# A graph kernel's first stage: last rank round cut short, layer norm moved to VectorE, triangles moved to Pool, order planned anew

## The chip, the cores and the metric

The kernel runs on one core of one Trainium2 chip. The metric is the device time of one execution in microseconds.

## What is computed

There are 16 graphs of 1024 nodes with 128 features each, a weighted adjacency matrix per graph and a node mask. Two layers follow each other, and each adds its result to x:

```python
h = jnp.maximum(_layernorm(x, axis=-1), 0.0)
x = x + L0(h, adj)               # three times: h = h@W+b; nh = h/|h|; cos = nh@nh.T; h = (adj*cos)@h; relu but for the last
h = jnp.maximum(_layernorm(x, axis=-1), 0.0)
x = x + L1(h, adj, nodemask)     # three graph convolutions with adj * keep, batch norms, a last product

def step(carry, n):              # keep comes from this scan over the 1024 rows of (adj > 0)
    row = jnp.take(carry, n, axis=0); nbi = row.astype(jnp.int32); num = jnp.sum(nbi)
    sf = jnp.where(num > T_DIL, (num + K_DIL - 1) // K_DIL, 1)      # T_DIL = 10, K_DIL = 2
    rm = row & (jnp.cumsum(nbi) % sf == 0)
    keep = ~jnp.where((mask_b[n] != 0) & (num > 1), rm, False)
    carry = carry.at[n].set(row & keep)
    carry = carry.at[:, n].set(carry[:, n] & keep)
```

The scan doesn't depend on x. It removes neighbours by rank, and each removal changes later rows.

## The kernel before

The first stage (`layer0`, lines 474 to 1021) does two things side by side.

**The convolutions.** 48 units (16 graphs times three products). Graphs go in pairs, two units alternating. A unit has 16 cosine steps and 16 aggregate steps, each on a half row block of 128x512: TensorE makes three cosine matmuls into one of two PSUM banks (lines 702 to 704), VectorE multiplies by the adjacency into one of four buffers (line 889), TensorE aggregates (line 711). Between them the next unit is prepared: for the first of a graph the layer norm, in three steps: `lna` (statistics on VectorE, lines 852 to 855, and a square root on ScalarE, line 759), `lnb` (reciprocal and -mean/deviation on VectorE, lines 859 and 861, then eight ScalarE instructions x*scale+bias, line 767), `lnc` (transposes on TensorE, line 639, and ReLU on ScalarE, line 778). For every unit then `ha` (line 683), `hb` (line 869), squares (line 784), `hc` (lines 873 and 789), `hd` (reciprocal, line 877, and eight ScalarE scalings, line 794), `hf` (transposes, line 639, and a copy, line 801), `ho` (line 881).

**The dilation.** The scan in blocks of 128 rows: 4 quads of 4 graphs, 8 blocks each, so 32 blocks n; two chains of 16 blocks (even and odd quads) run interleaved. In a block the removals of the diagonal 128x128 part are iterated a fixed number of rounds, `ROUNDS = [2, 3, 4, 6, 6, 3, 3, 8]` for the eight blocks (35 a quad). First the rows are loaded, ScalarE takes their sign (`row`, line 815), and a transposing DMA fills the slab T. `cross` (lines 921 and 925, VectorE) makes the matrix X from the triangle of the row block (Au) and from T. `base` counts (TensorE line 721, VectorE lines 939 and 941). A round r is: `rank` (TensorE line 734, into bank D0), `rule` (nine small VectorE instructions, lines 953 to 967), `rank` on ScalarE (four instructions, line 822), `drop` (VectorE, line 974), which writes one of the two buffers Sd. After the last round come `bias` (VectorE), eight `wide` steps (TensorE line 744 into bank D1, ScalarE line 832 into v, VectorE line 1006 into T), and `check` (line 1000), which compares the two Sd buffers and adds what differs to a flag; a flag above 0 starts a repair loop on the device, `dilate_all`. `flip` and `mask` (line 1018) make the keep matrix of a quad and store it.

**The order.** A planner (`Planner.order`) gets every step with engine, cost in ns, rank and predecessors (`plan_units`, `plan_dilation`), simulates all engines greedily (earliest start first, lower rank first) and writes one fixed order per engine. Each engine runs its list in that order and waits on semaphores at the head of its queue. Pool has no work in this stage. The second stage (lines 1256 on) follows after a barrier.

Of the kernel before, what the change touches and what calls it, by code (L numbers as in the profile page):

```python
# [9 lines left out]
BF16 = mybir.dt.bfloat16  # L10
# [3 lines left out]
ALU = mybir.AluOpType  # L14
# [23 lines left out]
ENGINES = ("pe", "act", "dve", "sp", "dma")  # L38
TAIL = {"pe": 60, "act": 130, "dve": 90, "sp": 0, "dma": 2000}
# [65 lines left out]
def build(nc, A):  # L105
    with ExitStack() as top:
# [7 lines left out]
        C["U2"] = sb("U2", [128, 132], BF16)  # L114
# [42 lines left out]
def setup(nc, A, C):  # L157
    with ExitStack() as ctx:
# [23 lines left out]
        def dve(e):  # L182
# [4 lines left out]
            e.memset(C["U2"][:], 1.0)  # L187
# [23 lines left out]
            e.tensor_scalar(C["U2"][:, 0:128], t[:, 1, :], 2.0, None, ALU.mult)  # L211
# [16 lines left out]
class Planner:  # L228
# [16 lines left out]
    def order(self, rings):  # L245
# [25 lines left out]
        for _ in range(len(steps)):  # L271
# [21 lines left out]
            if s.frees:  # L293
                ring, key = (s.frees, s.name) if s.frees in rings else (s.frees[0], s.frees)
                free[ring][held[(ring,) + key]] = s.end
# [20 lines left out]
def plan_units(P):  # L316
# [10 lines left out]
    def prepare(v):  # L327
# [4 lines left out]
        if i == 0:  # L332
# [17 lines left out]
        add("act", ("hd", v), 1610, 0, [("dve", "hd", v)])  # L350
# [14 lines left out]
    def agg(idx):  # L365
# [10 lines left out]
        if i == 2 and idx % 16 == 11:  # L376
            read = [("act", "lnb", G)] if g == G - 1 else []
            transfer(("xload", g), 1400, read + ([("dma", "postb", UNITS.index((g - 1, 2)))] if g else [("act", "lnb", 1)]))
# [10 lines left out]
    add("dve", ("lnb", G), 400, 1, [("act", "lna", G)])  # L389
    add("act", ("lnb", G), 1610, 1, [("dve", "lnb", G), ("pe", "hf", 3 * G - 1)])  # L390
    add("act", ("first", 0), 920, 3, [("act", "lnb", G)])
# [14 lines left out]
def plan_dilation(P):  # L406
# [3 lines left out]
    for n in sorted(range(QUADS * NK), key=lambda n: (n // NK // 2 * NK + n % NK, n // NK % 2)):  # L410
# [16 lines left out]
        if k:  # L427
# [3 lines left out]
        add("dve", ("cross", n), 1330, 5, ready + filled +  # L431
            ([("dve", "check", prev)] if done else []))
        add("pe", ("base", n), 700, 1, ready, None, "D1")
        add("dve", ("base", n), 320, 2, [("pe", "base", n)], None, None, "D1")
        for r in range(K):
            add("pe", ("rank", n, r), 260, 1, [("dve", "drop", n, r - 1)] if r else ready, None, "D0")
            add("dve", ("rule", n, r), 1140, 3, [("pe", "rank", n, r)] + ([] if r else [("dve", "base", n)] + done))
            add("act", ("rank", n, r), 1365, 1, [("dve", "rule", n, r)], None, None, "D0")
            add("dve", ("drop", n, r), 610, 3, [("act", "rank", n, r)] + ([] if r else [("dve", "cross", n)]))
        add("dve", ("bias", n), 700, 3, [("dve", "rule", n, K - 1)])  # L440
        add("dve", ("check", n), 610, 6, [("dve", "drop", n, K - 1)])
        for i in range(Q):
            for j in range(2):
                add("pe", ("wide", n, i, j), 330, 1, [("dve", "drop", n, K - 1)], None, "D1")
                add("act", ("wide", n, i, j), 960, 1, [("pe", "wide", n, i, j), ("dve", "bias", n)], None, "v", "D1")
                add("dve", ("wide", n, i, j), 605, 4, [("act", "wide", n, i, j)], None, None, "v")
        for m, j in FLIPS:
            if k == max(2 * m + 1, 4 * j + 3):
                for i in graphs_of(quad):
                    transfer(("flip", quad, i, m, j), 600, [("dve", "wide", quad * NK + b, i, m // 2)  # L450
                             for b in range(4 * j, 4 * j + 4)], "flip", "flip", rank=2)
                    for q in (2 * m, 2 * m + 1):
                        last = ("flip", quad, i, m, j) if q % 2 else None
                        add("dve", ("mask", quad, i, q, j), 620, 3, [("dma", "flip", quad, i, m, j),
# [19 lines left out]
def layer0(nc, A, C, S):  # L474
    with ExitStack() as ctx:
        P = Scope(nc, ctx, "a", C["bank"][0])
        E = P.sems("w xl xld xs tln relu ph hr sq cl nrm rn vn tnh nh nl cos ew agg ev tpost xadd "
                   "bst bag lnsd lnrs lnm lnr " + " ".join(f"adj{i}{k}" for i in range(2) for k in range(NK)))
        T = P.sems("at0 at1 fl0 fl1 fl2 fl3 af0 af1 af2 sign low au x bs b0 b1 ct ru vr sd v8 wb wd av rw kp kps0 kps1 kps2 sum tot flag")
# [14 lines left out]
        lnnm = P.sb("lnnm", [128, NK])  # L494
# [8 lines left out]
        Au = P.sb("Au", [128, Q, 128], FP8)  # L503
# [4 lines left out]
        cnt, quarter = ([P.sb(f"{n}{p}", [128, Q]) for p in range(2)] for n in ("cnt", "quarter"))  # L508
# [3 lines left out]
        small = P.sb("small", [128, 2, 8, Q])  # L512
        sm = [{n: small[:, p, x, :] for x, n in enumerate(("sf", "iv", "g", "sc", "va", "h", "c", "b2"))}
              for p in range(2)]
        D0, D1 = P.ps("D0", [128, Q, 128]), P.ps("D1", [128, Q, 128])
# [1551 lines left out]
```

## Time and profile before

| | us |
|---|---|
| median of 3 runs | 2694.39 |
| lowest and highest | 2693.61, 2701.42 |
| the profiled execution | 2693.11 |
| its span in the trace | 2691.3 |

The span is the time from the first to the last instruction; 1.8 us lie around it. Engines: PE is TensorE's matmuls, PEld its weight loads (they overlap PE), DVE is VectorE, ACT ScalarE, POOL GpSimd, SP the queue that issues the DMAs. A group of instructions has its line, engine, operation, output<-input names and shapes, count, then busy us and mean ns of one, then the idle time of the engine just before them and what ended it. Instructions of one engine overlap by some tens of ns, so that eight of them take less than eight times their mean.

### The profile page before, as it was taken

To read this page: it belongs to the slowest core of one execution; us is meant where nothing else is said; L and a number is where in the kernel's file an instruction comes from. 1 tells how busy PE (TensorE), PEld (TensorE's weight loads), DVE (VectorE), ACT (ScalarE), POOL (GpSimd) and SP (SyncE) were. 2 spreads that over 40 slices of the span, in tenths; PEclk is the share of its full clock that TensorE was granted. 3 is DMA by queue.
4 is the path that set the end of the run, shared out by engine and by line. 5 is a ranking of instruction groups with operands and counts; after the bars stand their busy time and mean duration, and the time that the engine had idled before them with its cause. 6 is when DMAs were issued, how large, how long until landed. Compare 5 with 4: busy or idle time off the path is not lost. (4 is left out here: it accounts for less than half of the span.)

```text
span 2691.3 us, 38914 instructions
## 1 busy us (share of the span) xinstructions
PE 2579.7 (96%) x12390; PEld 1630.3 (61%) x12390; DVE 2076.1 (77%) x5328; ACT 1459.3 (54%) x4324; POOL 562.7 (21%) x233
## 2 busy tenths in 40 slices
PE   6999999999999999899999998999999999999898
PEld 4666656656655666566666654555555555555897
DVE  4778889888988888888988877766666636776676
ACT  5667747766655776567656321322322344443676
POOL 0000000000000000000000002766666603433673
PEclk9999999999999999999999999999999999999999
DMA  7354275265367244536433323555555419996663
GB/s 235 89 148 147 57 187 156 65 160 167 77 170 220 83 136 133 128 100 192 114 112 120 83 69 140 195 191 192 193 192 192 182 55 384 404 402 263 249 233 153
DMA packets 325878, 455.48 MB, mean 169 GB/s; under 512 B 155680, under 2 KB 218528, under 8 KB 325664
## 3 DMA queue, kind: packets, MB, share of 16 engines
q1 hardware_dynamic: 325664, 452.89, 51.9%
q8 instruction: 102, 1.67, 0.3%
q14 instruction: 112, 0.92, 0.1%
HBM read 352.13 MB, written 67.11 MB: 156 GB/s over the span
## 5 line engine op out<-in xcount | busy, mean ns | idle before, releaser
L711 PE MATMUL a_acc<-a_ew,a_Hr 128*128 128x512 f32 x1536 | 751.9, 600 | 0.5 <-ACT a_hT L807 0.4
L889 DVE TENSOR_TENSOR a_ew<-adj,a_cos 128x512 f32<-128x512 f32 x768 | 508.6, 682 | 68.3 <-PE a_cos L704 66.0
L1720 POOL TENSOR_TENSOR b_dsum<-adj 128x1024 f32<-128x1024 f32 x15 | 133.3, 8885 | 1797.4 <-DVE adj L1628 1797.4
L702 PE MATMUL a_cos<-a_nh 128*128 128x512 f32 x768 | 413.3, 538 | 14.0 <-DVE a_ew L889 7.3
L711 PEld LDWEIGHTS a_acc<-a_ew,a_Hr 128*128 128x128 f32 x1536 | 275.2, 190 | 160.7 <-issue 112.2
L832 ACT ACTIVATE a_v<-a_D,a_wb,a_small 128x256 f16<-128x256 f32 x512 | 287.8, 635 | 86.4 <-PE a_D L744 84.5
L704 PE MATMUL a_cos<-a_nh,a_nl 128*128 128x512 f32 x768 | 304.1, 396 | 0.0
L703 PE MATMUL a_cos<-a_nl,a_nh 128*128 128x512 f32 x768 | 301.6, 393 | 0.0
L822 ACT ACTIVATE a_vr<-a_D,a_small 128x128 f16<-128x128 f32 x560 | 209.4, 456 | 135.3 <-DVE a_small L967 134.7
L1383 PE MATMUL b_acc<-adj,b_z 128*128 128x512 f32 x512 | 225.0, 592 | 0.0
L1480 PE MATMUL b_acc<-adj,b_z 128*128 128x512 f32 x512 | 222.5, 592 | 0.0
L815 ACT ACTIVATE a_Ab<-stage 128x512 fp8e4<-128x512 f32 x256 | 156.7, 633 | 111.2 <-DMA stage<-in_adj 110.5
L1724 POOL TENSOR_TENSOR b_dsum<-b_dsum,adj 128x1024 f32<-128x1024 f32 x90 | 211.4, 2349 | 12.9
L702 PEld LDWEIGHTS a_cos<-a_nh 128*128 128x128 f32 x768 | 145.5, 189 | 101.4 <-issue 44.1
L1018 DVE TENSOR_TENSOR a_kp<-a_T,stage 128x512 fp8e4<-128x512 fp8e4 x256 | 170.0, 686 | 41.4 <-DMA scr_keep<-a_kp 39.2
L1006 DVE SCALAR_TENSOR_TENSOR a_T<-a_v,a_Ab 128x512 fp8e4<-128x512 f16 x256 | 172.2, 685 | 29.0 <-ACT a_v L832 28.6
L703 PEld LDWEIGHTS a_cos<-a_nl,a_nh 128*128 128x128 f32 x768 | 146.3, 191 | 64.2 <-issue 51.4
L1480 PEld LDWEIGHTS b_acc<-adj,b_z 128*128 128x128 f32 x512 | 96.0, 190 | 114.3 <-issue 113.1
L704 PEld LDWEIGHTS a_cos<-a_nh,a_nl 128*128 128x128 f32 x768 | 144.7, 188 | 33.4
L1383 PEld LDWEIGHTS b_acc<-adj,b_z 128*128 128x128 f32 x512 | 94.8, 190 | 107.1 <-issue 107.1
L784 ACT ACTIVATE h<-a_Hr 128x128 f32<-128x128 f32 x384 | 113.1, 299 | 69.2 <-DVE a_Hr L869 69.1
L1515 ACT ACTIVATE b_z<-b_o 128x128 f32<-128x128 f32 x256 | 75.3, 297 | 116.9 <-DVE b_o L1699 100.6
(269 smaller groups left out, 4337.6 us busy)
## 6 DMA issues: line engine op xcount, KB each, us to landing
adj<-in_adjT SPq DMA_DIRECT2D x108, 1024.0 KB, 12.8
adj<-in_adjT SPq DMA_DIRECT2D x128, 512.0 KB, 4.3
stage<-in_adj SPq DMA_DIRECT2D x256, 256.0 KB, 3.3
scr_keep<-a_kp SPq DMA_DIRECT2D x256, 64.0 KB, 1.8
scr_z<-b_zT SPq DMA_DIRECT2D x32, 512.0 KB, 3.6
scr_ag<-b_a SPq DMA_DIRECT2D x32, 512.0 KB, 3.3
stage<-scr_keep SPq DMA_DIRECT2D x13, 1024.0 KB, 7.5
b_kp<-scr_keep SPq DMA_DIRECT2D x12, 1024.0 KB, 7.8
```

The costliest lines, as they stand in the source:

```text
L702: e.matmul(cos[j][:], n[:, blk(k)], n[:, half(j)], start=True, stop=False)
L703: e.matmul(cos[j][:], n[:, blk(k)], m[:, half(j)], start=False, stop=False)
L704: e.matmul(cos[j][:], m[:, blk(k)], n[:, half(j)], start=False, stop=True).then_inc(E["cos"], 1)
L711: e.matmul(acc[j][:], Hr[u % 2][:, k, :], ew[idx % EW][:], start=(k == 0), stop=(k == NK - 1)).then_inc(E["agg"], 1)
L822: e.activation(vr[p][:, i, :], D0[:, i, :], ACT.Abs, bias=sm[p]["b2"][:, i:i + 1], scale=sm[p]["sc"][:, i:i + 1]).then_inc(T["vr"], 1)
L832: t = e.activation(v[c % 3][:, g * 256:g * 256 + 256].rearrange("p (x s) -> p s x", s=2), D1[:, 2 * g:2 * g + 2, :], ACT.Abs, bias=wb[p][: ...
L889: e.tensor_tensor(ew[idx % EW][:], adj[g % 2][:, k, half(j)], cos[j][:], ALU.mult).then_inc(E["ew"], 1)
L1006: e.scalar_tensor_tensor(TT[:, slot, 2 * j:2 * j + 2, k].rearrange("p m x s -> p m (x s)"), v[c % 3][:].rearrange("p (m c) -> p m c", m=2) ...
L1018: e.tensor_tensor(as_blocks(kp[c % 3][:]), row_half(slot, j, q), turned[:, :, :, :, q % 2], ALU.mult, saturate=False).then_inc(T["kp"], 1)
L1383: t = e.matmul(acc[j][:], src[:, q, :], adj[n % 3][:, q, half(j)], start=(q == 0), stop=(q == NK - 1))
L1480: t = e.matmul(acc[j][:], z[m % 2][:, q, :], adj[slot(m)][:, q, half(j)], start=(q == 0), stop=(q == NK - 1))
L1724: e.tensor_tensor(d, d, b[:, q, :], ALU.add).then_inc(E["ds"], 1)
```

## The change

- The last round of a block has its rank product and its rule, but no ScalarE ranks and no removal: the rule's count and scale go straight into `wide`, which reads the Sd of the round before. `wide` needs the drop of round K-2; D0 is given back by the rule. The check runs after the block's wide steps: a new VectorE instruction makes the K-th Sd from the diagonal block of T that the wide step wrote, and the old instruction compares it with the other.
- `lnb`: the eight ScalarE instructions become eight VectorE `tensor_scalar` (subtract mean, multiply by 1/deviation); line 861 goes.
- The triangle (line 921) becomes a Pool `tensor_tensor`, with two buffers Au instead of one.
- U2 goes, UL stands in its place; `cnt` and `quarter` lie in `small`. The repair loop is adapted.
- The planner gets Pool as an engine and new costs: `lnb` 2280 ns on VectorE (before 400 there and 1610 on ScalarE), `hd` on ScalarE 2340 (1610), `row` 540 (620), `cross` 610 (1330) and `tri` 1250 on Pool, `check` 1220 (610), `mask` 605 (620). The orders of all engines come out anew.

```diff
-ENGINES = ("pe", "act", "dve", "sp", "dma")
-TAIL = {"pe": 60, "act": 130, "dve": 90, "sp": 0, "dma": 2000}
+ENGINES = ("pe", "act", "dve", "pool", "sp", "dma")
+TAIL = {"pe": 60, "act": 130, "dve": 90, "pool": 150, "sp": 0, "dma": 2000}
...
-            add("dve", ("lnb", g), 400, 1, [("act", "lna", g)])
-            add("act", ("lnb", g), 1610, 0, [("dve", "lnb", g)] + ([("pe", "hf", 0)] if g == 1 else []))
-            add("pe", ("lnc", g), 880, 0, [("act", "lnb", g)] + bank)
+            add("dve", ("lnb", g), 2280, 1, [("act", "lna", g)] + ([("pe", "hf", 0)] if g == 1 else []))
+            add("pe", ("lnc", g), 880, 0, [("dve", "lnb", g)] + bank)
...
-        add("act", ("hd", v), 1610, 0, [("dve", "hd", v)])
+        add("act", ("hd", v), 2340, 0, [("dve", "hd", v)])
...
-                add("act", ("row", n, i, j), 620, 2, [("dma", "row", n, i, j)], None, None, "af")
+                add("act", ("row", n, i, j), 540, 2, [("dma", "row", n, i, j)], None, None, "af")
...
-        add("dve", ("cross", n), 1330, 5, ready + filled +
-            ([("dve", "check", prev)] if done else []))
+        add("pool", ("tri", n), 1250, 1, [("act", "row", n, i, k // 4) for i in range(Q)] +
+            ([("dve", "cross", prev)] if done else []))
+        add("dve", ("cross", n), 610, 5, ready + filled + [("pool", "tri", n)] + ([("dve", "check", prev)] if done else []))
...
-            add("act", ("rank", n, r), 1365, 1, [("dve", "rule", n, r)], None, None, "D0")
-            add("dve", ("drop", n, r), 610, 3, [("act", "rank", n, r)] + ([] if r else [("dve", "cross", n)]))
+            if r < K - 1:
+                add("act", ("rank", n, r), 1365, 1, [("dve", "rule", n, r)], None, None, "D0")
+                add("dve", ("drop", n, r), 610, 3, [("act", "rank", n, r)] + ([] if r else [("dve", "cross", n)]))
...
-        add("dve", ("check", n), 610, 6, [("dve", "drop", n, K - 1)])
+        add("dve", ("check", n), 1220, 6, [("dve", "wide", n, i, k // 4) for i in range(Q)])
...
-                add("pe", ("wide", n, i, j), 330, 1, [("dve", "drop", n, K - 1)], None, "D1")
+                add("pe", ("wide", n, i, j), 330, 1, [("dve", "drop", n, K - 2)], None, "D1")
...
+        def pool(e):
+            for kind, *a in plan["pool"]:
+                n, = a
+                k, p, prev = n % NK, n // NK % 2, block_before(n)
+                e.wait_ge(T["sign"], max(nth["act", "row", n, i, k // 4] for i in range(Q)))
+                if prev is not None:
+                    e.wait_ge(T["x"], nth["dve", "cross", prev])
+                mine = Ab[:, slots(n), 256 * (k // 2):256 * (k // 2) + 256].rearrange("p i (x s) -> p i x s", s=2)
+                e.tensor_tensor(Au[p][:], mine[:, :, :, k % 2], C["tri"][:].unsqueeze(1).to_broadcast([128, Q, 128]),
+                                ALU.mult, saturate=False).then_inc(T["au"], 1)
...
-                    for k in range(NK):
-                        t = e.activation(tmp[:, k, :], x[:, k, :], ACT.Identity, bias=lnnm[:, k:k + 1],
-                                         scale=lnrs[:, k:k + 1])
...
-                    e.scalar_tensor_tensor(lnnm[:], lnmv[:, :, 0], -1.0, lnrs[:], ALU.mult, ALU.mult).then_inc(E["lnm"], 1)
+                    if g in (1, G):
+                        e.wait_ge(E["tnh"], 3 * g if g == G else 1)
+                    for k in range(NK):
+                        t = e.tensor_scalar(tmp[:, k, :], x[:, k, :], lnmv[:, k, 0:1], lnrs[:, k:k + 1],
+                                            ALU.subtract, ALU.mult)
+                    t.then_inc(E["lnr"], 1)
...
-                    e.wait_ge(T["sd"], nth["dve", "drop", n, ROUNDS[n % NK] - 1])
+                    k, p, c = n % NK, n // NK % 2, nth["dve", "check", n]
+                    e.wait_ge(T["rw"], max(nth["dve", "wide", n, i, k // 4] for i in range(Q)))
+                    e.wait_ge(T["ct"], nth["pe", "rank", n, ROUNDS[k] - 1])
+                    e.scalar_tensor_tensor(Sd[p][ROUNDS[k] % 2][:], TT[:, slots(n), k // 2, k, :, k % 2], 0.0, X[p][:],
+                                           ALU.is_equal, ALU.is_lt, saturate=False).then_inc(T["again"], 1)
```

## Rows read from the trace of the kernel before

**Rows 1.** The page: busy time by engine, and granted clock in 40 slices.
```profile
PE 2579.7 (96%) x12390; PEld 1630.3 (61%) x12390; DVE 2076.1 (77%) x5328; ACT 1459.3 (54%) x4324; POOL 562.7 (21%) x233
...
PEclk9999999999999999999999999999999999999999
```

**Rows 2.** Busy time by stretch: PE, PEld, DVE, ACT, POOL, clock, DMA share, GB/s.
```profile
0.00:30.18 30.18, 7.69 (x32) 6.62 (x33) 7.93 (x44) 13.47 (x40) 1.54 (x9) 1.00 0.82 302
30.18:1626.60 1596.42, 1539.72 (x7690) 978.94 (x7690) 1358.15 (x3645) 1004.94 (x2803) 0.00 (x0) 1.00 0.46 127
1626.60:2691.30 1064.70, 1032.28 (x4668) 644.75 (x4668) 710.05 (x1639) 440.87 (x1481) 561.19 (x224) 0.99 0.61 228
```

**Rows 3.** Waits of PE in 0 to 1625 us: total us, times, longest us.
```profile
PE a_pp L639 <- ACT h L767: 25.6, 16, 12.0
PE a_pp L639 <- ACT h L794: 18.7, 16, 7.0
PE a_D L744 <- ACT a_v L832: 11.4, 8, 3.6
PE a_cos L702 <- DVE a_ew L889: 7.3, 10, 1.3
PE a_cos L702 <- DVE a_nl L881: 6.0, 9, 2.4
PE a_D L721 <- DVE a_T L905: 2.5, 2, 1.3
...
PE a_D L734 <- DVE a_Sd L974: 0.8, 3, 0.3
```

**Rows 4.** Groups of instructions of the first stage, by line.
```profile
L889 DVE TENSOR_TENSOR a_ew<-adj,a_cos 128x512 f32<-128x512 f32 x768 | 508.6, 682 | 68.3 <-PE a_cos L704 66.0
...
L815 ACT ACTIVATE a_Ab<-stage 128x512 fp8e4<-128x512 f32 x256 | 156.7, 633 | 111.2 <-DMA stage<-in_adj 110.5
...
L974 DVE SCALAR_TENSOR_TENSOR a_Sd<-a_vr,a_X 128x512 fp8e4<-128x512 f16 x140 | 96.1, 686 | 27.0 <-ACT a_vr L822 26.8
...
L767 ACT ACTIVATE h<-h,a_lnnm,a_lnrs 128x128 f32<-128x128 f32 x120 | 47.8, 481 | 22.1 <-DVE a_lnnm L861 22.1
...
L921 DVE SCALAR_TENSOR_TENSOR a_Au<-a_Ab,tri 128x512 fp8e4<-128x512 fp8e4 x32 | 21.9, 685 | 0.9 <-DMA a_T<-a_Ab 0.9
```

**Rows 5.** Instructions in order of time, the start: start us, us, instruction, [idle before].
```profile
8.52 0.17 DVE L861 SCALAR_TENSOR_TENSOR a_lnnm<-a_lnmv,a_lnrs 128x8 f32<-128x8 f32 x1
8.72 3.18 ACT L767 ACTIVATE h<-h,a_lnnm,a_lnrs 128x128 f32<-128x128 f32 x8 [0.47 <-DVE a_lnnm L861]
...
11.96 1.97 PE L639 MATMUL a_pp<-ident,h 128*128 128x128 f32 x8 [11.96 <-ACT h L767]
```

**Rows 6.** Instructions in order of time, three places of the steady part.
```profile
651.41 3.19 ACT L767 ACTIVATE h<-h,a_lnnm,a_lnrs 128x128 f32<-128x128 f32 x8 [2.32 <-DVE a_lnnm L861]
654.50 1.48 ACT L822 ACTIVATE a_vr<-a_D,a_small 128x128 f16<-128x128 f32 x4
...
654.65 1.09 PE L639 MATMUL a_pp<-ident,h 128*128 128x128 f32 x8 [1.22 <-ACT h L767]
...
1584.77 2.45 ACT L794 ACTIVATE h<-a_Hr,a_rnrn 128x128 f32<-128x128 f32 x8 [1.09 <-DVE a_rnrn L877]
```

**Rows 7.** Instructions in order of time, VectorE in the second stage.
```profile
1656.72 2.14 DVE L1614 TENSOR_SCALAR xt<-xt,b_lnmv,b_lnrs 128x128 f32<-128x128 f32 x8
1658.78 9.16 DVE L1628 TENSOR_TENSOR adj<-adj,b_kp 128x1024 f32<-128x1024 f32 x8
```

**Rows 8.** Single lines of the second stage: duration ns min/median/max, first and last start.
```profile
L1679 DVE TENSOR_TENSOR b_rm<-b_rnrn,mf x16: 167/1970/1973, 1673.3 to 2173.1; 128x8 f32<-128x8 f32 x16
...
L1720 POOL TENSOR_TENSOR b_dsum<-adj x15: 8875/8882/8942, 1661.2 to 2133.5; 128x1024 f32<-128x1024 f32 x15
...
L1724 POOL TENSOR_TENSOR b_dsum<-b_dsum,adj x90: 2338/2348/2397, 1670.3 to 2154.9; 128x1024 f32<-128x1024 f32 x90
```

**Rows 9.** Instructions in order of time: two long waits of TensorE.
```profile
348.03 1.97 PE L639 MATMUL a_pp<-ident,h 128*128 128x128 f32 x8 [3.17 <-ACT h L794]
...
544.54 0.63 ACT L815 ACTIVATE a_Ab<-stage 128x512 fp8e4<-128x512 f32 x1 [4.22 <-DMA stage<-in_adj]
...
547.74 0.49 PE L744 MATMUL a_D<-UL,a_T 128*128 128x256 bf16 x4 [3.20 <-ACT a_v L832]
```

**Rows 10.** Busy time by stretch, columns as in rows 2.
```profile
345.00:350.00 5.00, 1.97 (x9) 1.85 (x10) 3.47 (x6) 3.97 (x11) 0.00 (x0) 0.75 0.53 132
```

**Rows 11.** The check's line, columns as in rows 8.
```profile
L1000 DVE SCALAR_TENSOR_TENSOR a_Au<-a_Sd x32: 682/685/693, 66.6 to 1488.3; 128x512 fp8e4<-128x512 fp8e4 x32
```

More of the change, by code:

```diff
@@ L113, in build @@
         C["tri"] = sb("tri", [128, 128], FP8)
-        C["U2"] = sb("U2", [128, 132], BF16)
         C["UL"] = sb("UL", [128, 512], BF16)
@@ L293, in order @@
             if s.frees:
-                ring, key = (s.frees, s.name) if s.frees in rings else (s.frees[0], s.frees)
+                ring, key = (s.frees, s.name) if s.frees in rings else s.frees
                 free[ring][held[(ring,) + key]] = s.end
@@ L376, in agg @@
         if i == 2 and idx % 16 == 11:
-            read = [("act", "lnb", G)] if g == G - 1 else []
-            transfer(("xload", g), 1400, read + ([("dma", "postb", UNITS.index((g - 1, 2)))] if g else [("act", "lnb", 1)]))
+            read = [("dve", "lnb", G)] if g == G - 1 else []
+            transfer(("xload", g), 1400, read + ([("dma", "postb", UNITS.index((g - 1, 2)))] if g else [("dve", "lnb", 1)]))
     transfer(("xfirst", 1), 1400, (), "sp")
@@ L452, in plan_dilation @@
                     for q in (2 * m, 2 * m + 1):
-                        last = ("flip", quad, i, m, j) if q % 2 else None
-                        add("dve", ("mask", quad, i, q, j), 620, 3, [("dma", "flip", quad, i, m, j),
+                        last = ("flip", ("flip", quad, i, m, j)) if q % 2 else None
+                        add("dve", ("mask", quad, i, q, j), 605, 3, [("dma", "flip", quad, i, m, j),
                             ("dve", "wide", quad * NK + q, i, j)], f"flip{quad}{i}{m}{j}", "kp", last)
@@ L502, in layer0 @@
         Ab = P.sb("Ab", [128, 2 * Q, N], FP8)
-        Au = P.sb("Au", [128, Q, 128], FP8)
+        Au = [P.sb(f"Au{p}", [128, Q, 128], FP8) for p in range(2)]
         X = [P.sb(f"X{p}", [128, Q, 128], FP8) for p in range(2)]
@@ L515, in layer0 @@
         D0, D1 = P.ps("D0", [128, Q, 128]), P.ps("D1", [128, Q, 128])
+        cnt, quarter = ([small[:, p, x, :] for p in range(2)] for x in (8, 9))
         mv4 = C["mv"][:].rearrange("p (g k) -> p g k", k=NK)
@@ L652, in take @@
                         e.wait_ge(T["b0"], nth["dve", "base", a[0]])
+                    elif kind == "rank" and a[1] == ROUNDS[a[0] % NK] - 1:
+                        e.wait_ge(T["ru"], 9 * nth["dve", "rule", a[0], a[1]])
                     elif kind == "rank":
@@ L857, in dve @@
                     g, = a
+                    x = xt if g in (1, G) else tmp
                     e.wait_ge(E["lnsd"], g + 1)
@@ L1019, in dve @@
                                     saturate=False).then_inc(T["kp"], 1)
-        run(nc, pe, act, dve, None, sp)
+        run(nc, pe, act, dve, pool, sp)
 def dilate_all(nc, A, C, S):
@@ L1045, in rule @@
             m = mv[:, k:k + 1]
-            e.tensor_tensor(cnt[:], Dp[:, 0, 128:129], base[:, 1:2], ALU.add).then_inc(E["rule"], 1)
+            e.scalar_tensor_tensor(cnt[:], Dp[:, 0, 128:129], 0.5, base[:, 1:2], ALU.mult, ALU.add).then_inc(E["rule"], 1)
             e.wait_ge(E["rule"], t0 + 1)
@@ L1070, in recount @@
             e.wait_ge(E["sd"], 1)
-            e.matmul(Dp[:, 0, 0:129], Sd[:], C["U2"][:, 0:129], start=True, stop=True).then_inc(E["rank"], 1)
+            e.matmul(Dp[:, 0, 0:129], Sd[:], C["UL"][:, 0:129], start=True, stop=True).then_inc(E["rank"], 1)
         with nc.Fori(0, G) as g:
@@ L1111, in pe @@
                                  start=(q == others[0]), stop=(q == others[-1]))
-                    e.matmul(Dp[:, 0, 0:129], AT[:, k, blk(k)], C["U2"][:, 0:129], start=True,
+                    e.matmul(Dp[:, 0, 0:129], AT[:, k, blk(k)], C["UL"][:, 0:129], start=True,
                              stop=True).then_inc(E["rank"], 1)
```

59 lines of the change are left out of this document (21 added, 38 removed).

## The prediction

> **What bounds the kernel now.** I read the page first: TensorE is busy 96% of the span, the other engines far less, and the granted clock is at its upper level nearly all the time [rows 1]. The change touches only the first stage, so the next view is the busy time by stretch: it cuts the run into the start, the steady part of the first stage (from the first cosine product at 30.18 us to the last store's transposes at 1626.6 us) and the rest [rows 2]. In the steady part TensorE works 1539.7 of 1596.4 us. The change adds no matmul and removes none: the ranks of the last round stay, and the move from U2 to UL keeps the same 128 columns. So what it can win is in the 56.7 us in which TensorE stands still there, plus the start, where it works 7.7 of 30.2 us. Third, the waits of TensorE by line [rows 3]. They say which engine was late: the transposes (L639) waited 25.6 us for the layer norm's output from ScalarE (L767) and 18.7 us for the normalised rows (L794). The wide products (L744) waited 11.4 us for L832. VectorE is behind the cosine waits, 7.3 and 6.0 us. The longest of these waits, 12.0 and 7.0 us and 2.4 of the cosine waits on L881, are the start. Steady, L767 costs 25.6 - 12.0 = 13.6 us in 15 waits, L794 18.7 - 7.0 = 11.7 us in 15. The rest of the first stage is bound by TensorE's own work, and everything after 1626.6 us is untouched.
>
> **Why those waits are there.** All engines of this stage follow orders that a planner wrote from its own costs, so a step that takes longer than its cost is waited for at the head of TensorE's queue. The layer norm's second half is entered at 400 ns on VectorE and 1610 ns on ScalarE, but the eight ScalarE instructions take 3.19 us [rows 6], 1.58 more. At 651 us they end at 654.6 and the transposes start then, after 1.22 us of standing still [rows 6]; an average wait of 13.6 / 15 = 0.9 us fits a shortfall of 1.58. L794 is also entered at 1610 ns and takes 2.45 us [rows 6], 0.84 short.
>
> **The change, part by part.**
> Start. The first layer norm is a bare chain. Now the small product at 8.52 us is followed by 3.18 us on ScalarE and TensorE starts at 11.96 [rows 5]. After, eight VectorE instructions with two per-row scalars follow the reciprocal, where the small product stood. The same instruction form with the same shapes stands in the second stage: eight in 2.14 us [rows 7]. Start 8.52, end 10.66, TensorE at about 10.75: **-1.2 us**. One conversion of U2 and one fill less in the setup: 0 to -0.15, take -0.1.
>
> Layer norm, steady. On ScalarE 17 x 3.19 = 54 us go [rows 4, 6]. On VectorE 17 x 2.14 = 36.4 us come, less 17 small products of 0.17 (one at the start is in [rows 5]), 2.9 us. The new entry, 2280 ns, is near 0.20 + 0.04 + 2.14 = 2.38 us, so the shortfall of 1.58 falls to 0.1. The order can then put cosine and aggregate products ahead of the transposes. Bounds: 0 back (the wait only changes its name) to 13.6 back. I take **-11**, since the cause is one constant error that is repaired.
>
> The hd entry, 1610 to 2340 ns. It alone repairs the L794 waits. Of the 11.7 us, 3.17 come from one wait in another situation (a ScalarE instruction behind a late load, below), so 8.5 are open. Bounds 0 and 8.5; I take **-6.5**.
>
> Last round without ranks and removal. Each of the 32 blocks loses four ScalarE instructions (4 of them in 1.48 us at 654.5 us [rows 6]): 47 us of ScalarE in all, and one removal of 0.69 us on VectorE [rows 4], 22 us. The check gets it back as one more instruction of the same shape, 22 us: nothing on VectorE. The chain of a block gets shorter by 1.48 + 0.69 + two crossings, about 2.3 us; 16 blocks follow each other in either of the two chains, so the last check, now at 1488 us [rows 11], comes up to 37 us earlier. Nobody on TensorE waits for it: the stage ends with the aggregates at 1626 us. Worth 0 by itself. The wide products can start before the last rule is done but their reader L832 can't, so D1 may be held about 1.5 us longer by the first of eight. That touches base products and other wide products that share D1. Bounds: 32 x 1.5 = 48 us of a held bank if TensorE always stood in front of it, and below nothing, since ScalarE, with 101 us less to do, is late less often. TensorE's waits on L832 are 11.4 us in 8, with two of 3.2 and 3.6 us. The one of 3.2 us: ScalarE waits 4.22 us for a load of adjacency rows, then L832 comes late, then L744 [rows 9]. Such waits come from loads, not from ScalarE's work, and a new order deals them anew; I leave them in number. They also cost clock: after the 3.17 us wait before 348 us [rows 9] the granted clock of the stretch is 0.75 [rows 10], that is part of it at the lower level of 1.2 GHz. For the smaller waits on L832 I take **-1**.
>
> Triangles on Pool. VectorE loses 32 x 0.684 = 21.9 us (L921) [rows 4]. Pool gets 32 instructions of 512 elements a partition. The nearest row is its two-input instruction on 1024 f32 elements, 2.35 us [rows 8]: half is 1.2 us. They start when the row signs are there and the crossing also waits for transposes behind those signs, so the result is early; Pool does nothing else in this stage. The price is elsewhere. In the second stage the small VectorE product L1679, with both inputs in SBUF, takes 0.17 us at least but 1.97 us in the median, where Pool is at work, and Pool's L1720 takes 8.9 us, not 2.35, as the eight products L1628 of two SBUF tiles run on VectorE [rows 7, 8]. So each triangle can hold VectorE for up to 1.2 us: 38 us in all. L889, 508.6 us [rows 4], has one operand in PSUM, and VectorE is idle 238 us of the steady part [rows 2]; together that is 47% of the time, so about half of the triangles meet something they hold, about 20 us. That eats what L921 gave back.
> The Trainium skill, page "SBUF — State Buffer", section "Who interferes with whom", speaks against this part: the pair of ports that VectorE and GpSimd share is an exclusive lock, and an instruction with two SBUF inputs, or a `tensor_scalar` in a two-port mode, blocks in full against a GpSimd instruction that reads SBUF. The rows just named agree with it ([rows 8]). By that rule the new layer norm instructions can be held too; the time it would give is rival 3's, worked out there from rows alone.
>
> VectorE as a whole: +36.4 - 2.9 - 21.9 = +11.6 us of work, and about 20 us of holding, on 1358 of 1596 us [rows 2]: from 85% to 87%. What TensorE pays for VectorE now is 7.3 + (6.0 - 2.4) + 2.5 + 0.8 = 14.2 us steady [rows 3]. A layer norm step now blocks the queue for 2.4 us in one piece, ahead of the element products L889 that free the cosine banks; there are 768 of them in 1596 us, one in 2.08, each 0.68 us, so a block of 2.4 us is 1.0 more than the 1.4 between two of them. Bounds: 0, and 38 + 16 x 1.0 = 54 us. From the row it is nearest to (14.2 us paid at 85% load) I take **+5**.
>
> **Sum.** -1.2 - 0.1 - 11 - 6.5 - 1 + 5 = -14.8 us. The profiled execution took 2693.1 us (span 2691.3 and 1.8 around it), the median of the runs is 2694.4. Rounded for what a new order spoils, I take -14: **2680 us**, 0.5% faster. A measurement of this kernel tells 0.3%, 8 us, from no change.
>
> **Rivals.**
> (1) The forecast, 2672 to 2686 us: chance 0.48.
> (2) The waits change their names. The two repaired entries take 17 us of waiting away, but the new order meets its own late loads and late L832, as at 348 and 547 us [rows 9]. One such wait of 3.4 us with its slow clock (about 2 us more) is 5.5; two more of them and a cost of 5 to 10 us on VectorE give back 16 to 21, so 2688 to 2697. For it: ScalarE stood idle 111 us before its row signs, for loads [rows 4], and no entry for loads is changed. Against it: the average of such waits needn't grow. Chance 0.27.
> (3) Slower: Pool's triangles and the 2.4 us blocks hold L889. Place: VectorE's queue, where a held two-SBUF instruction stands ahead of an element product. Price: up to 38 us for the triangles and 16 for the blocks, against 20 won: at most +34, and at half of the price (27) plus two late loads (11) +18, 2712 us. It decides from about 0.9 us of each triangle reaching TensorE (32 x 0.9 = 29, against 20 won and past the 8 that can be told). Against it: VectorE is idle 15% of the time and four buffers of products lie between. Chance 0.11.
> (4) More: the stage closes up. With 101 us less on ScalarE and truer costs (the row entry goes from 620 to 540 ns too) most of the 56.7 us goes: 35 of it and 1.3 at the start, 2694 - 36 = 2658 us; partly, 2665. Chance 0.14.
> That the change doesn't do what it says: the check compares the same two rounds as before, so if nothing was unsettled before, nothing is now; otherwise the repair loop would run and cost far over 10%. Chance under 0.01, left out.
>
> **How the numbers follow.** Likeliest 2680. The forecast's own range is 2672 to 2686; to hold 8 in 10 it takes in rival 2 and the edges of 3 and 4: **2665 to 2698**. Faster by over 0.3% (below 2686.3): all of 1 and 4, 0.62. Within 0.3% (2686.3 to 2702.5): rival 2 and a little of 3, 0.29. Slower (above 2702.5): the rest of 3, 0.09.
>
> **What would show it.** In the profile after: the waits of L639 on the layer norm under 4 us steady and on L794 under 5; TensorE's first instruction near 10.8 us; ScalarE's first-stage work down by about 100 us; VectorE's up by 12 us plus held instructions (its two-SBUF instructions with maxima near 1.8 us); Pool with 32 instructions of about 1.2 us; the last check before 1460 us; the second stage unchanged at 1064.7 us. Wrong would be: waits of L702 on L889 over 20 us (rival 3), waits of L744 on L832 over 20 us (rival 2, or D1 held), or a second stage that moves by more than 3 us.

## The result and the profile after

The changed kernel takes 2690.7 us (median of 19 runs, 2683.4 to 2695.4), the kernel before 2696.6 in the same 19 rounds. The ratio is 0.998, 95% interval 0.9972 to 0.9987: 5.4 us faster (3.5 to 7.5), where 14 were forecast. Carried over to the 2694.4 us that the forecast started from, that is 2689 us. It lies inside the range of 2665 to 2698 us, but in rival 2's stretch, the one that the forecast called no change, and outside the likeliest case's 2672 to 2686. The interval leaves 1 out, so this pair of orders does differ, by less than half of the forecast. Of the kernel before's 19 executions one took 8152 us; such slow ones are left out of every ratio. The profiled execution has a span of 2684.3 us, 7.0 below that of before.

By stretch (columns as in rows 2), the answer to [rows 2]:

```profile
0.00:28.82 28.82, 7.70 (x33) 6.63 (x33) 9.45 (x49) 10.29 (x32) 1.55 (x9) 0.86 0.82 306
28.82:1621.56 1592.74, 1535.18 (x7690) 983.19 (x7691) 1378.35 (x3725) 915.66 (x2547) 36.80 (x32) 0.99 0.47 128
1621.56:2684.30 1062.74, 1031.57 (x4668) 644.91 (x4668) 695.15 (x1639) 439.99 (x1481) 560.46 (x224) 0.99 0.60 229
```

The start is 1.4 us shorter, the steady part 3.7 (1596.4 before), the rest 2.0. ScalarE works 89 us less in the steady part, VectorE 20 us more, Pool 36.8 us for 32 triangles. But TensorE stands still for 1592.7 - 1535.2 = 57.6 us there, against 56.7 before. The waits show what filled the place (TensorE, 0 to 1625 us: total us, times, longest), the answer to [rows 3]:

```profile
PE a_cos L712 <- DVE a_ew L895: 16.4, 16, 2.1
PE a_cos L712 <- DVE a_nl L887: 14.8, 10, 3.0
PE a_D L754 <- ACT a_v L832: 11.5, 14, 2.3
PE a_pp L647 <- DVE h L865: 11.5, 2, 10.6
PE a_pp L647 <- ACT h L794: 8.6, 6, 7.0
PE a_D L744 <- DVE a_Sd L974: 7.8, 12, 1.2
PE a_D L731 <- DVE a_T L911: 2.5, 4, 1.6
PE a_D L731 <- DVE a_T L915: 1.8, 3, 0.9
```

Without the start (10.6, 7.0 and 2.4 us of these), the waits for the layer norm are 0.9 us where 13.6 stood, those for L794 1.6 where 11.7 stood: 22.8 us went. The waits for VectorE, for element products, the low part nl, removals and T, are 16.4 + 12.4 + 7.8 + 2.5 + 1.8 = 40.9 where 14.2 stood: 26.7 us came. The start is the bare chain that was forecast (VectorE, then TensorE, in order of time), the answer to [rows 5]:

```profile
8.39 2.14 DVE L865 TENSOR_SCALAR h<-h,a_lnmv,a_lnrs 128x128 f32<-128x128 f32 x8
...
10.59 1.97 PE L647 MATMUL a_pp<-ident,h 128*128 128x128 f32 x8 [10.59 <-DVE h L865]
```

Two places show VectorE late (VectorE, Pool and TensorE in order of time). In the first a crossing, 0.69 us elsewhere, takes 1.58 us beside a triangle on Pool. The element products and nl stand behind it, and TensorE waits 3.03 us, of which the hold is 0.9:

```profile
1068.34 1.34 POOL L641 TENSOR_TENSOR a_Au<-a_Ab,tri 128x512 fp8e4<-128x512 fp8e4 x1 [26.12 <-ACT a_Ab L815]
...
1068.65 1.58 DVE L925 SCALAR_TENSOR_TENSOR a_X<-a_T,a_Au 128x512 fp8e4<-128x512 fp8e4 x1
1070.16 1.27 DVE L895 TENSOR_TENSOR a_ew<-adj,a_cos 128x512 f32<-128x512 f32 x2
1071.35 1.21 DVE L887 TENSOR_TENSOR a_nl<-a_pp,a_nh 128x1024 fp32r<-128x1024 f32 x1
...
1072.62 0.80 PE L712 MATMUL a_cos<-a_nh 128*128 128x512 f32 x1 [3.03 <-DVE a_nl L887]
```

In the second the new check, two instructions in one step, stands ahead of nl:

```profile
423.30 0.69 DVE L998 SCALAR_TENSOR_TENSOR a_Sd<-a_T,a_X 128x512 fp8e4<-128x512 fp8e4 x1
424.02 0.69 DVE L1004 SCALAR_TENSOR_TENSOR a_X<-a_Sd 128x512 fp8e4<-128x512 fp8e4 x1
...
424.64 1.22 DVE L887 TENSOR_TENSOR a_nl<-a_pp,a_nh 128x1024 fp32r<-128x1024 f32 x1
...
425.91 0.50 PE L712 MATMUL a_cos<-a_nh 128*128 128x512 f32 x1 [1.97 <-DVE a_nl L887]
```

### The profile page after: what moved, and what is told of

Read it like the earlier page. It is cut to its first block and busy times, and to the rows that moved or that the text cites. A ratio compares the mean times of both kernels' runs of the same rounds, so it can differ in the third digit from the quotient of the medians.

```text
span 2684.3 us, 38830 instructions
## 1 busy us (share of the span) xinstructions
PE 2574.4 (96%) x12390; PEld 1634.7 (61%) x12390; DVE 2082.9 (78%) x5413; ACT 1365.9 (51%) x4060; POOL 598.8 (22%) x265
## 5 line engine op out<-in xcount | busy, mean ns | idle before, releaser
L895 DVE TENSOR_TENSOR a_ew<-adj,a_cos 128x512 f32<-128x512 f32 x768 | 508.0, 681 | 69.0 <-PE a_cos L714 67.1
L712 PE MATMUL a_cos<-a_nh 128*128 128x512 f32 x768 | 417.2, 543 | 31.5 <-DVE a_ew L895 16.4
L641 POOL TENSOR_TENSOR a_Au<-a_Ab,tri 128x512 fp8e4<-128x512 fp8e4 x32 | 36.8, 1150 | 1367.2 <-ACT a_Ab L815 1367.2
L832 ACT ACTIVATE a_v<-a_D,a_wb,a_small 128x256 f16<-128x256 f32 x512 | 287.2, 632 | 99.8 <-PE a_D L754 59.9
L822 ACT ACTIVATE a_vr<-a_D,a_small 128x128 f16<-128x128 f32 x432 | 161.9, 457 | 134.1 <-DVE a_small L967 133.8
```

The costliest lines, as they stand in the source:

```text
L712: e.matmul(cos[j][:], n[:, blk(k)], n[:, half(j)], start=True, stop=False)
L822: e.activation(vr[p][:, i, :], D0[:, i, :], ACT.Abs, bias=sm[p]["b2"][:, i:i + 1], scale=sm[p]["sc"][:, i:i + 1]).then_inc(T["vr"], 1)
L832: t = e.activation(v[c % 3][:, g * 256:g * 256 + 256].rearrange("p (x s) -> p s x", s=2), D1[:, 2 * g:2 * g + 2, :], ACT.Abs, bias=wb[p][: ...
L895: e.tensor_tensor(ew[idx % EW][:], adj[g % 2][:, k, half(j)], cos[j][:], ALU.mult).then_inc(E["ew"], 1)
```

## The experiments

Theory A: the repaired waits are a real gain, and VectorE's new load gave most of it back. Theory B: a new order deals the waits anew, whatever the parts do. Each ratio is to the kernel before, run beside it. Any change of a cost makes the planner write all orders anew; such an order is called a deal below. Three runs (f1 to f3) keep an order as it stands instead. The steady part of each run, from its first cosine product to its last transposes, is called its units.

**What a new order alone is worth.** One planner constant, in the kernel before (l1, l2) and in the changed one (l3, l4):

```diff
-SIGNAL = 100
+SIGNAL = 105      # l1, l3; 95 in l2, l4
```

> The kernel before with the planner's signal time at 105 ns for 100, nothing else: the same instructions and nearly the same costs, but the greedy planner deals another order. It measures what a new order alone is worth. Theory B (much of every difference here is the deal of the order): off the kernel before by 0.3% or more either way (8 us). Theory A (differences come from what is moved and from costs): within 0.15%.

> The kernel before with signal time 95 ns. Theory B: off by 0.3% or more, and not by the same as with 105. Theory A: within 0.15% of before.

> The changed kernel with signal time 105 ns. Theory B: off the changed kernel (0.998) by 0.3% or more. Theory A: ratio 0.9965 to 0.9995.

> The changed kernel with signal time 95 ns. Theory B: off 0.998 by 0.3% or more, with the last mask anywhere between 1560 and 1640 us. Theory A: ratio 0.9965 to 0.9995.

Measured: l1 1.0044 (1.0027 to 1.0060), l2 1.0077 (1.0060 to 1.0093), l3 0.9957 (0.9941 to 0.9973), l4 0.9973 (0.9962 to 0.9983). The same instructions in another order cost 12 and 21 us. The old order is the best of its three deals, and theory B holds for it. The three deals of the changed kernel lie within 0.23%, less than theory B's 0.3%, though l3 lies just below theory A's 0.9965. The means are 1.0040 and 0.9970, 0.7% or 19 us apart. No deal of one side reaches the other's, but three a side are few: luck alone would part them in this way in one case of 20. In l2 the waits for the layer norm and L794 are there as in before (14.8 and 9.6 us), with 17.0 on L832.

**Costs alone.** e1 is the kernel before with four entries changed and no instruction moved, g3 the same with signal time 105 ns. The two entries not shown are `row` 540 and `mask` 605.

```diff
-            add("act", ("lnb", g), 1610, 0, ...
+            add("act", ("lnb", g), 3060, 0, ...
-        add("act", ("hd", v), 1610, 0, [("dve", "hd", v)])
+        add("act", ("hd", v), 2340, 0, [("dve", "hd", v)])
```

> The kernel before with nothing but truer planner costs: hd 2340 for 1610 ns, the layer norm's ScalarE half 3060 for 1610, row 540 for 620, mask 605 for 620; every instruction is that of before, only the orders are new. Theory A (the change gained through repaired costs, and VectorE's new load gave it back): the two waits of L639, 25 us steady before, fall under 6 and little comes back, 2679 to 2685 us, ratio 0.993 to 0.996. Theory B (a repaired wait returns under another name whatever carries it, since the new order deals the rest anew): the steady waits of TensorE sum to 45 to 60 us as before, ratio 0.998 to 1.001.

> The kernel before with true costs alone, second deal (105 ns). The first gave 1.0105. If true costs are worse in themselves: 1.007 to 1.013. If they are neutral against other deals of before (1.0044, 1.0077 and the kernel before itself, 1): 1.000 to 1.008. If the forecast's step holds (repaired entries gain 17 us): 0.993 to 0.998.

Measured: e1 1.0105 (1.0091 to 1.0120), g3 1.0098 (1.0070 to 1.0125), slower than every other deal of before, g3 as expected if true costs are worse in themselves. Theory A's expectation of 0.993 to 0.996 failed by 1.4%, and theory B's of 0.998 to 1.001 too. The two repaired waits did fall, to 2.1 and 6.0 us in e1, and came back with interest (TensorE in the units of e1; 2.4 us of the nl line are the start):

```profile
PE a_D L744 <- ACT a_v L832: 23.3, 17, 3.8
PE a_cos L702 <- DVE a_nl L881: 17.4, 10, 2.4
PE a_cos L702 <- DVE a_ew L889: 10.6, 16, 1.7
PE a_D L734 <- DVE a_Sd L974: 10.4, 12, 3.0
PE a_pp L639 <- ACT h L794: 6.0, 6, 2.8
```

TensorE waits 40.2 us for VectorE here, and 40.9 in g3, where it waits 14.2, 21.0 and 24.6 us in the three deals of before. VectorE's work is that of before. So the costs alone bring the waits for VectorE that the changed kernel shows (40.9).

**One entry back.** e5 is the changed kernel with the hd entry at 1610 again.

> The changed kernel with the one cost entry hd back at 1610 ns. Theory A (the repaired entry takes 8 to 10 us of waits away): L647 waits for L794 rise from 2 to 9 us or more in the steady part, ratio 0.999 to 1.002. If truer costs spoil more than they mend (before with true costs alone was 1.0%, and up to 0.6% worse than other orders of before): ratio 0.994 to 0.997. Theory B: 0.995 to 1.000 with no tie to the waits of L794.

Measured: 0.9967 (0.9954 to 0.9980), overlapping the changed kernel's own deals, and this (TensorE, from 28.9 us; 2.4 us of the nl line are the start):

```profile
PE a_pp L647 <- ACT h L794: 15.9, 23, 1.6
PE a_D L754 <- ACT a_v L832: 9.6, 12, 2.0
PE a_cos L712 <- DVE a_ew L895: 7.6, 10, 1.8
PE a_cos L712 <- DVE a_nl L887: 5.4, 5, 2.4
```

The wait for L794 is back as theory A expected, 15.9 us for 1.6 (3.5 and 1.5 in l3 and l4), but the ratio is not 0.999 to 1.002: it lies in the range for true costs that spoil more than they mend. The waits for nl and the element products are 10.6 us, where the changed kernel's three deals have 28.8, 20.7 and 17.0. L794, L801, L887 and the next unit's first cosine are one chain: with the transposes planned later, TensorE's wait goes from the chain's middle to its end. That fits these rows; it wasn't measured by itself.

**The layer norm.** f2 keeps the order of before; g5 and g6 (signal time 105) plan anew with the move alone; e2 and g1 (signal time 105) are the changed kernel with it back on ScalarE, -mean/deviation in `lnsd`.

```diff
# f2, g5, g6: on VectorE, after the reciprocal (g5, g6: one step of 2280 ns)
-                        t = e.activation(tmp[:, k, :], x[:, k, :], ACT.Identity, bias=lnnm[:, k:k + 1],
-                                         scale=lnrs[:, k:k + 1])
+                        t = e.tensor_scalar(tmp[:, k, :], x[:, k, :], lnmv[:, k, 0:1], lnrs[:, k:k + 1],
+                                            ALU.subtract, ALU.mult)
# e2, g1: the reverse in the changed kernel
-            add("dve", ("lnb", g), 2280, 1, ...
+            add("dve", ("lnb", g), 400, 1, [("act", "lna", g)])
+            add("act", ("lnb", g), 3060, 0, ...
```

> The order of the kernel before as it stands, but the layer norm's eight instructions are VectorE's, at the place of its small product; ScalarE's step is empty. The forecast's step (the waits of L639 on the layer norm go, 11 us, at little cost): ratio 0.995 to 0.997. If a 2.15 us block that the order didn't reckon with delays the element products: the 13 us come back as waits of L702, ratio 0.999 to 1.002.

> The kernel before with only the layer norm's move to VectorE and its cost of 2280 ns, planned anew. With the old order kept the move cost 0.23%. If the order has to reckon with the block for the gain to come, and the true value is 11 us against a typical deal of before (mean 1.004): ratio 0.997 to 1.002. If the move alone is worth nothing: 1.002 to 1.008.

> The kernel before with only the layer norm's move to VectorE, planned anew, second deal (105 ns). If a part has a value of its own, it repeats the first deal within 0.3%; if everything is the deal, it differs by 0.4% or more.

> The changed kernel with the layer norm's second half back on ScalarE, entered at its true 400 + 3060 ns. Theory A: the 36 us of VectorE blocks were what cost the wait for L881/L887 and the element products; without them these waits (28 us steady after the change) fall by about 10 us, 2682 to 2687 us, ratio 0.994 to 0.997. Theory B: within 0.15% of the changed kernel, ratio 0.997 to 1.000.

> The changed kernel with the layer norm's half back on ScalarE (true costs), second deal: signal time 105 ns. The first deal gave 1.0056. If the layer norm's place is worth its 0.8% in itself, this lies at 1.003 to 1.008, above all three deals of the changed kernel (0.9957 to 0.9980). If the first was a bad deal: 0.997 to 1.001.

Measured: f2 1.0023 (1.0014 to 1.0032), g5 1.0086 (1.0060 to 1.0112), g6 1.0082 (1.0064 to 1.0100), e2 1.0056 (1.0042 to 1.0070), g1 1.0011 (0.9996 to 1.0026). In f2 the waits for the layer norm went, but TensorE's wait of L734 for removals rose from 0.8 to 13.6 us, not those of L702 as expected: a block that the order doesn't reckon with. g5 looks like a loss and isn't one on TensorE (stretches of g5, columns as in rows 2):

```profile
28.98:1614.54 1585.56, 1539.38 (x7691) 980.83 (x7691) 1370.17 (x3729) 959.28 (x2675) 0.00 (x0) 0.99 0.45 126
1625.00:1650.00 25.00, 0.00 (x0) 0.00 (x0) 12.69 (x20) 0.00 (x0) 0.00 (x0) 0.50 0.37 92
```

Its units take 1585.6 us (g6: 1585.8), 10.9 less than before (l1 and l2: 1612.7 and 1619.8), and end at 1614.5. Then TensorE stands idle: VectorE still makes masks, the last at 1649.6 us, and the second stage's first VectorE instruction comes at 1658.8, where before had 1583.9 and 1635.5. A second path reaches the barrier, the dilation's; with the layer norm alone it ends last. The last check shows where it lost time: 1583.4 and 1585.8 us in g5 and g6, 1488.3, 1516.7 and 1544.5 in the three deals of before. g6 repeats g5 within 0.3%, but both lie above the 0.997 to 1.002 that a gain would have shown, since no expectation had this path. Back on ScalarE in the changed kernel the layer norm costs 0.3 to 0.8% in two deals (g1 lies between its two expectations); the units then take 1613.9 and 1598.9 us where the changed kernel's deals take 1592.2 to 1595.4, so its worth on TensorE shows from both sides. e2 missed both its expectations (0.994 to 0.997 and 0.997 to 1.000): taking the 2.15 us blocks off VectorE gained nothing.

**The short last round.** f3 keeps the order of before; e4 and g2 (signal time 105) are the changed kernel with the full round, the check's single comparison again behind the last removal.

```diff
# e4, g2 in the changed kernel
-            if r < K - 1:
-                add("act", ("rank", n, r), 1365, 1, [("dve", "rule", n, r)], None, None, "D0")
-                add("dve", ("drop", n, r), 610, 3, ...
+            add("act", ("rank", n, r), 1365, 1, [("dve", "rule", n, r)], None, None, "D0")
+            add("dve", ("drop", n, r), 610, 3, ...
-                add("pe", ("wide", n, i, j), 330, 1, [("dve", "drop", n, K - 2)], None, "D1")
+                add("pe", ("wide", n, i, j), 330, 1, [("dve", "drop", n, K - 1)], None, "D1")
```

> The order of the kernel before as it stands, without the last round's four ScalarE ranks and its removal; the check's instruction stays in its place but compares one Sd with itself and its result isn't used, so this kernel leaves the check out. It measures the shorter chain and 47 + 22 us less work with no new order. The forecast gave this 0 to -1 us: ratio 0.998 to 1.000. If the shorter chain is the gain that the variant with the full round pointed to (0.6% between it and the changed kernel): ratio 0.993 to 0.996.

> The changed kernel with the last round's four ScalarE ranks and its removal on VectorE restored, and the check's single comparison after it. Theory A: ScalarE has 47 us more to do, TensorE's waits on L832 (11.5 us) grow by a few us: ratio 0.998 to 1.001. If the check, now 1.4 us in one piece after the wide steps, is what delays the cosine chain on VectorE, this is faster, 0.995 to 0.997. The last check comes at 1488 us or later in the first case.

> The changed kernel with the full last round, second deal (105 ns). The first gave 1.0041, with the last mask at 1641 us, 20 us after TensorE's units: the dilation's chain set the stage's end. If the short last round is worth keeping the chain off the end, the last mask comes after 1615 us again and the ratio is 1.000 to 1.006. If that was the deal: last mask before 1600 and 0.996 to 0.999.

Measured: f3 0.9979 (0.9970 to 0.9988), e4 1.0041 (1.0028 to 1.0054), g2 1.0061 (1.0039 to 1.0083). f3's 6 us lie between both expectations; its profiled execution shows none of it (steady part 1597.4 us), so where they are stays open. e4 is slower than either of its expectations, and g2's masks end after 1615 us as expected. These two decide. TensorE's units take 1592.70 us in both, as in the changed kernel (1592.74): on TensorE the short round is worth nothing. But look at the mask's line (last start is the number before the semicolon) and the first VectorE instruction of the second stage: first changed kernel, then e4, then g5.

```profile
L1022 DVE TENSOR_TENSOR a_kp<-a_T,stage x256: 636/685/1418, 335.0 to 1573.3; 128x512 fp8e4<-128x512 fp8e4 x128
1630.05 0.17 DVE L1648 MEMSET onesf<- 128x128 f32 x1 [6.13 <-issue]
```

```profile
L1015 DVE TENSOR_TENSOR a_kp<-a_T,stage x256: 636/684/1501, 336.4 to 1640.9; 128x512 fp8e4<-128x512 fp8e4 x128
1649.38 0.17 DVE L1641 MEMSET onesf<- 128x128 f32 x1 [7.78 <-issue]
```

```profile
L1012 DVE TENSOR_TENSOR a_kp<-a_T,stage x256: 639/689/697, 342.2 to 1649.6; 128x512 fp8e4<-128x512 fp8e4 x128
1658.79 0.17 DVE L1638 MEMSET onesf<- 128x128 f32 x1 [8.53 <-issue]
```

With the full round the masks end 68 us later, 20 us behind the units, and the second stage starts 19 us later (g2: masks to 1645.3). The last check comes at 1566.9 and 1579.6 us in e4 and g2, at 1524.5 to 1534.3 in the changed kernel's three deals. So the short round is what lets the layer norm's move count.

**The triangle.** f1 keeps the order of the changed kernel and has VectorE make the triangle ahead of the crossing; e3 and g7 (signal time 105) plan anew. f1's order reckons with 610 ns on VectorE at that place, and the two instructions take 1.4 us.

```diff
# e3, g7 (f1 keeps the planned order)
-        add("pool", ("tri", n), 1250, 1, ...
-        add("dve", ("cross", n), 610, 5, ...
+        add("dve", ("cross", n), 1330, 5, ready + filled + ([("dve", "check", prev)] if done else []))
```

> The order of the changed kernel as it stands, instruction for instruction, but the triangle is made by VectorE at the place of the crossing and Pool does nothing. No new order, so only the place of the triangle is measured. If the hold through Pool costs more than the work: faster than the changed kernel, ratio 0.995 to 0.997. If the 22 us of VectorE work are worth more (rows of the changed kernel show only about 10 us of held instructions): ratio 1.000 to 1.003, that is 5 to 13 us over it. Theory B (what moves the time is the deal, parts are small): within 0.15% of 0.998.

> The changed kernel with the triangle back on VectorE (cost 1330 as before). If the hold through Pool's triangle costs more than the 22 us of work that it takes off VectorE, this is faster than the changed kernel: ratio 0.995 to 0.997, and VectorE's maxima fall to 0.69 us. If the move was worth its work, it is slower: ratio 0.999 to 1.002. Theory B expects no difference beyond 0.15% from 0.998.

> The changed kernel with the triangle on VectorE, planned anew, second deal (105 ns). The first deal gave 0.9958, the changed kernel 0.998, but with the changed kernel's order kept, the triangle on VectorE cost 0.3%. If the first deal was luck: 0.998 to 1.003. If the triangle is better on VectorE once the order reckons with it: 0.994 to 0.997.

Measured: f1 1.0012 (1.0002 to 1.0021), 0.32% or 8.6 us over the changed kernel; its steady part is 1600.4 us, 7.7 longer. e3 0.9958 (0.9946 to 0.9971), g7 1.0014 (1.0003 to 1.0025). By their expectations f1 says that the move was worth its work, e3 the opposite, and g7 that e3 was luck. In the order that was planned for Pool the triangle is better on Pool. With new orders TensorE sees no difference: the units take 1597.0 and 1592.5 us with the triangle on VectorE, 1592.7, 1595.4 and 1592.2 with it on Pool. What differs is the second path. The masks of e3 and of g7:

```profile
L1027 DVE TENSOR_TENSOR a_kp<-a_T,stage x256: 636/684/695, 331.0 to 1621.3; 128x512 fp8e4<-128x512 fp8e4 x128
```

```profile
L1027 DVE TENSOR_TENSOR a_kp<-a_T,stage x256: 640/686/694, 331.8 to 1628.9; 128x512 fp8e4<-128x512 fp8e4 x128
1637.87 0.17 DVE L1653 MEMSET onesf<- 128x128 f32 x1 [8.28 <-issue]
```

They end at 1621 and 1629 us, where the changed kernel's three deals have 1573.3, 1576.1 and 1587.8. In g7 that is 7.6 us behind the units, and its second stage starts 8 us later than the changed kernel's: about the 9 us of their ratios (1.0014 and 0.998). e3 and l3 (0.9957) are the fastest measured, but e3's second deal shows that as a draw of the order, not as a better design.

**All deals side by side.** Every kernel with an order of its own, in us of its profiled execution: how long TensorE stands idle in its units, what of it are waits for L794 and for VectorE (the layer norm apart), and where the last mask lies against the end of the units (minus: ahead of it).

| kernels | hd entry | layer norm | idle | for L794 | for VectorE | last mask |
|---|---|---|---|---|---|---|
| before, l1, l2 | 1610 | ScalarE | 56.7, 67.1, 73.6 | 11.7, 16.3, 9.6 | 14.2, 21.0, 24.6 | -43, -69, -39 |
| g5, g6 | 1610 | VectorE | 46.2, 49.7 | 6.4, 9.4 | 18.3, 15.5 | +35, +35 |
| e5 | 1610 | VectorE | 53.4 | 15.9 | 16.1 | -5 |
| e1, g3 | 2340 | ScalarE | 78.8, 73.0 | 6.0, 4.2 | 40.2, 40.9 | -33, -29 |
| e2, g1 | 2340 | ScalarE | 71.0, 57.2 | 1.7, 2.0 | 42.1, 25.1 | -75, -53 |
| changed, l3, l4 | 2340 | VectorE | 57.6, 54.2, 55.8 | 1.6, 3.5, 1.5 | 40.9, 26.4, 30.9 | -48, -48, -33 |
| e4, g2 | 2340 | VectorE | 54.8, 57.0 | 1.9, 6.1 | 33.0, 24.9 | +20, +24 |
| e3, g7 | 2340 | VectorE | 56.6, 53.9 | 3.1, 0.8 | 31.6, 36.1 | -4, +8 |

The waits for VectorE go with the hd entry: at 1610 they are 14.2 to 24.6 us in six deals, at 2340 they are 24.9 to 42.1 us in eleven, wherever the layer norm and the triangle are. The idle time is shorter with the layer norm on VectorE. With the entry it goes the other way than forecast, if by little: with the layer norm on VectorE it is 46.2 to 53.4 us at 1610 and 53.9 to 57.6 at 2340, though only e5 differs from the changed kernel by the entry alone. So neither theory holds as stated. Of the repaired waits the layer norm's were a real gain and L794's were not, and it was the entry, not VectorE's load, that gave them back.

## Why the prediction was off, point by point

- **Start: right.** -1.3 forecast, -1.4 measured; eight instructions in 2.14 us, TensorE at 10.59 us against 10.75.
- **Layer norm, steady: right as a term.** -11 forecast. The waits fell by 12.7 us, and with the move alone (g5, g6) the units took 10.9 and 10.6 us less than in the kernel before, and 27 or more less than in l1 and l2.
- **hd entry: the step that failed.** -6.5 us forecast, on the sentence "It alone repairs the L794 waits." It does: they fell by 10.1 us. But TensorE gained nothing by it. The waits for VectorE rise when only cost entries change (e1, g3: 40.2 and 40.9 us, with VectorE's old work), and they are low when only the hd entry is put back (e5: 16.1 us, with all of VectorE's new work). Between e5 and the changed kernel's three deals the idle time of TensorE is 1 to 4 us longer with the true entry. The runs support the bound of 0 or a little less, not the choice.
- **VectorE's price: mis-sized, and for another reason.** +5 forecast, +26.7 us measured on the waits for VectorE (14.2 to 40.9); over the means of three deals a side it is +12.8 (19.9 to 32.7). The bounds, 0 to 54, held it; the choice, "from the row it is nearest to", did not. That row was a mean price at 85% load, and it was carried over to 87%. The load wasn't the cause: the 2.15 us block alone leaves these waits at 18.3 and 15.5 us (g5, g6). What raised them is the hd entry, by the eleven deals with it against the six without, of which only e5 is a single swap; that it does so by the later transposes, which put nl in front of TensorE, is the likely link and not shown. How much the check in one piece and the held instructions add isn't shown; e4 and g2, whose check is a single comparison, have 33.0 and 24.9 us.
- **Sum of the steady part.** -12.7 - 10.1 + 26.7 + 0.8 (L832) = +4.7 us; smaller waits and gaps that no wait names are 3.8 us fewer, so TensorE stands still 0.9 us longer. Its matmuls took 4.5 us less time (1539.7 to 1535.2). Together -3.7 us. The 4.5 us were not forecast; stretches of reduced granted clock differ between executions, and they weren't separated. One execution each doesn't carry so fine a sum: f3 and f2, in the order of before, have 1539.3 and 1542.9 us of matmuls.
- **Short round "worth 0 by itself": right on TensorE, wrong for the kernel.** The sentence "Nobody on TensorE waits for it" looked at one path to the end of the stage. In the kernel before the masks ended 43 us ahead of the units, so the second path wasn't seen; in e4, g2, g5 and g6 they end 20 to 35 us behind them.
- **The last check: wrong.** Before 1460 us was forecast, from 16 shorter blocks; it comes at 1530 us. Against the same kernel with the full round (1566.9 and 1579.6 us) the last check of the changed kernel's three deals does come 33 to 55 us earlier, where up to 37 was forecast. What the forecast left out is that the layer norm on VectorE delays the dilation, whose steps queue there: 1583 to 1586 us in g5 and g6, 1488 to 1545 in the deals of before. The last mask is 11 us earlier than before.
- **Triangle: the hold was over-priced.** Forecast: 20 us of holding against 22 of work, nothing. Pool's triangle takes 1.10 us, and the mean durations show about 10 us of held instructions (the new L998 760 ns where 685 is its median). f1 gives the move 8.6 us, in an order that was planned for it; with new orders it is worth nothing on TensorE, as forecast, and 33 to 56 us on the last mask (two deals against three; e5, with it on Pool, has 1613.8 us). That VectorE is held by a Pool instruction, which the Trainium skill's page "SBUF — State Buffer", section "Who interferes with whom", states as a lock, agrees with the 1.58 us crossing above; the price is half of the bound used.
- **The comparison itself.** The kernel before was measured in one order, the best of three deals; deals 5% of a constant away are 12 and 21 us slower. The forecast took 0.8 us for "what a new order spoils". Mean against mean the change is worth 19 us, more than the 14 forecast; that the measured pair gives 5 is in part the luck of a good old order. Rival 2 (the waits change their names) was right in size and sign; its carrier was VectorE's queue, not late loads.

Open: by what link the true hd entry makes VectorE late; why true costs alone are slower than all other deals of before in both deals (1.0105, 1.0098), where the waits for L832 are up too, at 23 us; and the 6 us of f3.

## What to carry to other kernels

Where every engine runs a planned order, a new plan is a change of its own: before a change is priced at 0.5%, measure two or three neighbouring orders of both kernels, or keep the order and swap only the instructions. A wait that a wrong cost entry explains isn't yet a gain; follow the chain behind it to the next instruction that the busiest helper engine must do. And list every path that reaches the stage's end, with its slack: a part that is worth nothing on the bounding engine can be what keeps the second path from becoming the bound. Waits of one execution pair mix the part with the deal; the same sum over several deals told here which part they belong to.

## What the runs showed of the hardware

A Pool `tensor_tensor` on 512 fp8 elements a partition takes 1.10 us (half of the 1024-element f32 one, 2.35 us [rows 8], is 1.17), up to 1.56 beside VectorE; VectorE instructions of 0.17 and 0.69 us take up to 1.05 and 1.59 us in the changed kernel; with Pool idle (f1) the mask's longest is 0.70 us, not 1.42. While TensorE idles for 25 us at the end of the stage in g5, the mean granted clock of the stretch is 0.50, the 1.2 GHz level.
